# A feed-forward stage in which the rotation of latent keys moves to VectorE in 18 pieces, the norms are spread over three tiles, and the second part of a hidden tile is made in that tile's own turn

## The chip, the cores and the metric

The program runs on one core of a Trainium2 chip. The metric is the device time of one execution in microseconds (us). The engines are TensorE (PE, with its weight loads PEld), VectorE (DVE), ScalarE (ACT), GpSimd (POOL) and the DMA queues of SyncE (SP).

## The reference, cut to what matters

The kernel computes two decoder layers for 16 sequences of 128 tokens with 256 features. Each layer has an attention, a cross attention and a feed-forward part, each followed by an addition and a layer norm:

```python
x = _layernorm(x + _L0_attn_ref(x, ...))
x = _layernorm(x + _L0_xattn_ref(x, ctx_512, ctx_512))
x = _layernorm(x + _L0_ffn_ref(x, w_gate, w_up, w_down, s_gate, s_up, s_down))
x = _layernorm(x + _L1_attn_ref(x, ...))
x = _layernorm(x + _L1_xattn_ref(x, ctx_512, ...))
x = _layernorm(x + _L1_ffn_ref(x, ...))
```

The change is in the third line, the feed-forward of layer 0, whose weights are int8 with a scale for each output column:

```python
gate = silu(x @ w_gate * s_gate)      # 256 -> 1024
up   = x @ w_up * s_up
y    = (gate * up) @ w_down * s_down  # 1024 -> 256
```

While this stage runs, the kernel also prepares an input of a stage far behind it, the fifth line. There the latent context is rotated before it serves as keys and as values:

```python
kv_rope = kv_c * cos[None] + _rotate_half(kv_c) * sin[None]   # 16 x 128 x 64
```

It is made twice, once with the features on the partitions (`mla_keys`, 128 x 2048) and once with the tokens there (`mla_values`, 128 x 1024).

## The kernel before

**Tiles.** `gated_ffn_int8` works in 32 tiles (`TILES`). The sequences form 4 groups of 4 (512 token columns), and the 1024 hidden features form 8 tiles (`FT`) for each group. Tile n has these steps:
- `up(n)` on TensorE (L768): 16 matmuls, 8 for the gate and 8 for up. The input is held as two parts whose sum is x (`x_parts`), so each product is made of two.
- `silu(n)` on ScalarE (L690).
- `fuse(n)` on VectorE (L726): up, scaled, times gate, into one of two buffers `fused`. It reads one operand from PSUM and one from SBUF.
- `hidden_first(n)` on ScalarE (L695): the hidden tile rounded to the matmul's type, the first part of `h_parts`.
- `hidden_second(n)` on VectorE (L731): what the rounding left over, the second part. It reads two operands from SBUF.

**Order of the engines.** Each engine runs its own loop over n, up to `END` = 42, in the order in which it is written, and waits on semaphores. TensorE writes the gate and up products to two PSUM buffers each, so `up(n)` waits for `silu(n - 2)` and `fuse(n - 2)`. ScalarE does `silu(n)`, then `hidden_first(n)`, which waits for `fuse(n)`, and only then `silu(n + 1)`. VectorE does `fuse(n)` and then `hidden_second(n - 1)`, the second part of the tile before.

**Sequences.** When a group's 8 tiles are done, the down product (L780, 16 matmuls of 256 columns) of each of its sequences b is made, one in every second tile: `begins(b)` is 9, 11, 13, ... 39. In VectorE's turn `begins(b) + 1`, an even one, `scale_and_add` scales it (L619), adds the residual (L167), takes the statistics (L171, L172, L173) and forms variance plus epsilon (L174). GpSimd raises that to the power -1/2 (L188), VectorE waits for it and normalises (L181), all in the same turn. GpSimd then adds a bias into `x_tok` (L194), TensorE transposes the normalised rows (L200) and ScalarE copies them to `xT` (L205), these two in their turn `begins(b) + 3`. The last sequence, 15, is finished in the next stage.

**Splits.** For groups 1 to 3 the input's parts are made in tiles 3, 11 and 19 by ScalarE (`split_first`, L685) and at the end of VectorE's turns 4, 12 and 20 (`split_second`, L720).

**What is left of the stage ahead.** In tiles 0 to 4 the last two sequences of the cross attention are finished. In turn 2 VectorE divides and forms the statistics of the last one, in turn 3 it normalises it.

**Rotation.** GpSimd does it after its share of the norms of sequences 0, 1, 2, 4, 6 and 8, in six instructions (L978, L980, L982, L984, L986, L988): `rotate_after(b)`, ahead of which it waits for its own `kept`. The inputs come by DMA into buffers that the cross attention has left.

## Time and profile before

| what | us |
|---|---|
| median of 3 runs | 1135.53 |
| lowest and highest of the 3 | 1128.24, 1140.06 |
| the profiled execution, its own time | 1127.11 |
| its span in the profile | 1125.0 |
| PE busy in the span | 1009.5 |
| DVE busy | 788.7 |
| ACT busy | 556.8 |
| POOL busy | 264.8 |

The profiled execution is a single run, a little under the lowest of the three. A row of the timeline gives the start of an instruction in us from the span's start, its duration, engine, line, operation, output and inputs, and in brackets how long the engine had been idle and what ended that. Durations in neighbouring rows overlap by some hundredths, since an instruction can begin while the one ahead drains. The distance from one start to the next is what an instruction takes from the queue. In the rows `rows` is the home of y, the total and the normalised rows, and `gqa_expT` is the home of gate and fused (and, in its other half, of the rotated copy of the keys).

### The profile page before, as it was taken

The page shows a single profiled execution, that of the slowest core. Times are in us where ns is not written, and L with a number is a line of the kernel's source. Part 1 is how long each engine was busy: PE and PEld are TensorE (multiplying, and loading weights), DVE is VectorE, ACT ScalarE, POOL GpSimd, SP SyncE. Part 2 cuts the span into 40 slices and gives each one's busy share as a digit, 9 for nine tenths or more (in the row PEclk, how much of TensorE's full clock was granted, in tenths as well). Part 3 has the DMA queues.
Part 4 walks back from the last instruction along what each step waited for, and adds up shares of the span by engine and source line. Part 5 has one row for each costly group of instructions (what it writes and reads, how often), then busy time and mean ns, then how long its engine had stood idle before and what let it go on. Part 6 is the DMA issues. An engine that isn't in the chain of part 4 may idle for free. (4 is left out here: it accounts for less than half of the span.)

```text
span 1125.0 us, 23649 instructions
## 1 busy us (share of the span) xinstructions
PE 1009.5 (90%) x8691; PEld 649.9 (58%) x8691; DVE 788.7 (70%) x1959; ACT 556.8 (49%) x1538; POOL 264.8 (24%) x331
## 2 busy tenths in 40 slices
PE   9799989999799999887979788899999998989975
PEld 5466666666333333576755476677777774444432
DVE  2689987898778777577757986744587877723326
ACT  2355436555366667533414264677777774322213
POOL 5301000221111112144331202300000001277843
PEclk9899999999899999999979989999999999999978
DMA  6923433000222221700000006910000002778567
GB/s 191 151 74 104 127 82 114 3 2 3 75 86 91 78 73 57 162 3 1 2 0 2 1 14 226 284 39 17 13 21 20 25 20 76 215 192 228 87 147 264
DMA packets 79197, 94.78 MB, mean 84 GB/s; under 512 B 17504, under 2 KB 61478, under 8 KB 78822
## 3 DMA queue, kind: packets, MB, share of 16 engines
q1 hardware_dynamic: 69356, 78.67, 24.0%
q0 software_dynamic: 6496, 9.57, 4.6%
q10 hardware_dynamic: 3232, 5.03, 1.3%
q8 instruction: 71, 1.16, 0.4%
q14 instruction: 42, 0.34, 0.1%
HBM read 68.65 MB, written 21.97 MB: 81 GB/s over the span
## 5 line engine op out<-in xcount | busy, mean ns | idle before, releaser
L540 DVE TENSOR_REDUCE gqa_x_slots<-banks 128x8 f32<-128x1024 f32 x64 | 78.3, 1225 | 29.5 <-PE banks L434 19.5
L500 ACT ACTIVATE gqa_expT<-banks 128x1024 f32<-128x1024 f32 x64 | 65.5, 1023 | 51.2 <-PE banks L455 51.2
L1735 ACT ACTIVATE mla_probs<-mla_scores,mla_neg_max 128x128 f32<-128x128 f32 x256 | 90.3, 384 | 0.1
L455 PE MATMUL banks<-gqa_x_slotsT,gqa_keys 32*128 32x512 f32 x256 | 73.4, 644 | 13.0 <-issue 4.0
L1808 DVE TENSOR_REDUCE mla_neg_max<-mla_scores 128x8 f32<-128x1024 f32 x32 | 39.2, 1224 | 64.7 <-PE mla_scores L1633 38.4
L434 PE MATMUL banks<-gqa_keys_bd,xT 32*128 32x512 f32 x256 | 72.3, 650 | 1.7 <-PEq L2739 1.4
L768 PE MATMUL banks<-ff_x_parts,ff_w_gate_up 128*128 128x512 f32 x256 | 66.6, 407 | 1.0 <-PEq L358 1.0
L1623 PE MATMUL mla_q_ps<-xT,mla_merged_home 128*128 128x128 f32 x512 | 62.4, 275 | 0.0
L1660 PE MATMUL mla_out_ps<-mla_merged_home,mla_attT 128*128 128x256 f32 x256 | 60.7, 380 | 0.7 <-ACT mla_attT L1749 0.7
L1623 PEld LDWEIGHTS mla_q_ps<-xT,mla_merged_home 128*128 128x128 f32 x512 | 59.7, 192 | 0.0
L1735 ACT ACTIVATION_READ_ACCUMULATOR mla_probs<-mla_scores,mla_neg_max 128x1 f32 x256 | 57.3, 224 | 0.0
L768 PEld LDWEIGHTS banks<-ff_x_parts,ff_w_gate_up 128*128 128x128 f32 x256 | 47.4, 194 | 11.4 <-issue 2.2
L188 POOL TENSOR_TENSOR mla_n_rstd<-mla_n_var_eps,neg_half 128x1 f32<-128x1 f32 x16 | 8.8, 548 | 190.7 <-DVE mla_n_var_eps L174 190.7
L2169 DVE COPY moe_y<-moe_y_ps 112x256 f32<-112x256 f32 x32 | 13.6, 424 | 57.1 <-PE moe_y_ps L2096 38.3
L2924 DVE SCALAR_TENSOR_TENSOR ttt_masked<-banks,ttt_mask 128x512 f32<-128x512 f32 x64 | 43.5, 684 | 12.6 <-PE banks L2845 12.5
L2055 POOL DMA_INDIRECT moe_sums<-moe_y,moe_rows_out x32 | 47.3, 1479 | 17.3 <-issue 8.2
L695 ACT CAST ff_h_parts<-gqa_expT 128x512 fp32r<-128x512 f32 x32 | 19.9, 621 | 62.1 <-DVE gqa_expT L726 62.1
L1660 PEld LDWEIGHTS mla_out_ps<-mla_merged_home,mla_attT 128*128 128x128 f32 x256 | 46.1, 190 | 6.5 <-ACT mla_attT L1749 1.6
L1270 DVE TENSOR_TENSOR bat_prod<-bat_k,ba_attended 128x128 f32<-128x128 f32 (+15 forms) x32 | 40.3, 1318 | 11.6 <-ACT bat_k L1181 7.5
L455 PEld LDWEIGHTS banks<-gqa_x_slotsT,gqa_keys 32*128 32x128 f32 x256 | 21.1, 187 | 46.7 <-issue 46.7
L1640 PEld LDWEIGHTS mla_turned<-ident,mla_probs 128*128 128x128 f32 x256 | 28.4, 141 | 28.1 <-issue 28.1
L2880 PEld LDWEIGHTS banks<-ttt_g_pairs,ttt_masked 128*64 128x64 f32 x1024 | 35.8, 137 | 11.4 <-issue 8.2
(460 smaller groups left out, 2543.8 us busy)
## 6 DMA issues: line engine op xcount, KB each, us to landing
gqa_keys_bd<-in_gqa_keys_bd SPq DMA_DIRECT2D x16, 512.0 KB, 3.2
moe_w_gu<-in_moe_w_gu SPq DMA_DIRECT2D x14, 384.0 KB
moe_w_dn<-in_moe_w_down SPq DMA_DIRECT2D x24, 192.0 KB
moe_sums<-moe_zeros SPq DMA_DIRECT2D x2, 2176.0 KB, 10.3
ba_attended<-in_moe_w_gu SPq DMA_DIRECT2D x10, 384.0 KB
x_tok<-in_mla_kv_wo SPq DMA_DIRECT2D x8, 320.0 KB, 3.7
ttt_by_token<-ttt_g_pairs SPq DMA_DIRECT2D x4, 576.0 KB, 5.1
ttt_lanes<-ttt_by_token SPq DMA_DIRECT2D x16, 144.0 KB
```

The lines of the kernel that those rows point to most:

```text
L434: ins = nc.tensor.matmul(scores[:, j, :], keep["xT"][group, c, b * T:(b + 1) * T], keys_bd[b % NBUF][group, c], start=True, stop=True)
L455: ins = nc.tensor.matmul(scoresT[:, j % 2, :], keys[b % NBUF][group, c, :], x_slotsT[group, k % 2, :], start=True, stop=True)
L500: nc.scalar.activation(expT[:, k % 2, 2 * u:2 * u + 2, :], scoresT, ACT.Exp, scale=HD ** -0.5).then_inc(exp_ready, 1)
L540: nc.vector.tensor_reduce(x_slots[:, b % 2, :, c * NJ + 2 * half:c * NJ + 2 * half + 2, HD].rearrange("p g j -> p j g"), scores[:, of].rea ...
L768: ins = nc.tensor.matmul(tile[:, n % 2], w_up[:, c, k, f * P:(f + 1) * P], x_parts[:, g % 2, part, c, :], start=(c == 0 and part == 0), st ...
L1270: tt(prod[:, u % PB, 0:l + 1, :], k[:, c, 0:l + 1, :], q[:, c, l, :].unsqueeze(1).to_broadcast([P, l + 1, T]), ALU.mult).then_inc(prod_rea ...
L1623: ins = nc.tensor.matmul(q_ps[:, i, :], to_keys[:, c, 2 * pair:2 * pair + 2, :], keep["xT"][:, c, b * T:(b + 1) * T], start=(c == 0), stop ...
L1660: ins = nc.tensor.matmul(out_ps, attT[:, k % 2, i, :], to_out[:, r * QP + i, :], start=(r == 0 and i == 0), stop=(r == UNITS - 1 and i == ...
L1735: ins = nc.scalar.activation(probs[:, k % NB, e, i, :], scores[:, k % 2, e, i, :], ACT.Exp, bias=neg_max[:, k % 2, e, i:i + 1], accum_out= ...
L1808: nc.vector.tensor_reduce(neg_max[:, k % 2], scores[:, k % 2], AX_X, ALU.max, negate=True).then_inc(max_kept, 1)
L2055: nc.gpsimd.indirect_dma_start(sums, bass.IndirectOffsetOnAxis(ap=rows_out[0:USED, s:s + 1], axis=0), y2[0:USED, s % 4, :], None, compute_ ...
L2924: stt(masked[:, u % NB].rearrange("p n j i -> p (n j) i"), scores[:, u % NB].rearrange("p n j i -> p (n j) i"), 1.0, mask[:].unsqueeze(1). ...
```

## The change

Four things are different, all in `gated_ffn_int8` and `LatentWeights`:
- GpSimd no longer rotates, and no longer waits for `kept` behind each norm. `LatentWeights.rotate` does it on VectorE in 18 pieces of 128 x 512 elements, one in each of the turns 11 to 28: twelve for the keys (cosine product, sine product, sum, for four sequences each) and six for the values.
- For sequences 0 to 11 (`LATE` = 12) the norm is spread over three turns of VectorE. Turn `begins + 1`: scale and add. Turn `begins + 2`: statistics, and the variance at its end. Turn `begins + 3`: normalise. The piece of the rotation and the second part stand between steps that depend on each other. Sequences 12 to 14 keep the whole norm in one turn.
- `hidden_second(n)` is in turn n, behind `fuse(n)`, and not in turn n + 1.
- The transposition on TensorE and the copy on ScalarE of sequences 0 to 11 come one turn later, in `begins + 4`, behind the down product of a later sequence. TensorE's row of transposition then stands between a down product and two tiles of `up`.

```diff
         def _(pool):
-            rotate_after = latent.gpsimd(pool)
...
                 norm.gpsimd(pool, b)
-                pool.wait_ge(norm.kept, b + 1)
-                rotate_after(b)
...
+        LATE = B - 4
+        turned_at = lambda n: next((b for b in range(B - 1) if begins(b) + (4 if b < LATE else 3) == n), None)
...
-                if sequence_at(n - 3) is not None:
-                    norm.scalar(act, sequence_at(n - 3))
+                if turned_at(n) is not None:
+                    norm.scalar(act, turned_at(n))
...
+            ROTATE_AT = FT + 3
+
+            def normalise(b):
+                need(dve, norm.rstd_ready, b + 1)
+                need(dve, norm.kept, b)
+                need(dve, norm.turn_ready, b)
+                nc.vector.tensor_scalar(norm.normed, norm.total, norm.mean_var[:, 0:1], norm.rstd[:], ALU.subtract, ALU.mult).then_inc(norm.norm_ready, 1)
...
-                b = sequence_at(n - 1)
+                b, was, before = (None if sequence_at(n - k) == B - 1 else sequence_at(n - k) for k in (1, 2, 3))
...
-                if 1 <= n <= TILES:
-                    hidden_second(n - 1)
...
-                    last.scale_and_add(dve, order, b, down[b % 2])
+                if before is not None and before < LATE:
+                    normalise(before)
+                if b is not None:
+                    dve.wait_ge(down_ready, b + 1)
+                    if b:
+                        order.after(added)
+                    nc.vector.tensor_tensor(last.y, down[b % 2], last.s_down[:], ALU.mult).then_inc(y_ready, 1)
+                if was is not None and was < LATE:
+                    order.after(added)
+                    summed = order.mark(nc.vector.bn_stats(norm.stats[:], norm.total))
+                if n == ROTATE_AT:
+                    dve.wait_ge(fetched, LOADS)
+                if ROTATE_AT <= n < ROTATE_AT + latent.PIECES:
+                    latent.rotate(dve, n - ROTATE_AT)
+                if was is not None and was < LATE:
+                    order.after(summed)
+                    nc.vector.memset(norm.spare[:], 0.0)
+                    spread = order.mark(nc.vector.bn_aggr(norm.mean_var[:], norm.stats[:]))
+                if b is not None:
...
+                    added = order.mark(norm.added(b, last.y))
+                if n < TILES:
+                    hidden_second(n)
+                if was is not None and was < LATE:
+                    order.after(spread)
+                    nc.vector.tensor_scalar(norm.var_eps[:], norm.mean_var[:, 1:2], LN_EPS, None, ALU.add).then_inc(norm.var_ready, 1)
+                if b is not None and b >= LATE:
+                    order.after(added)
+                    norm.vector_stats(order)
+                    normalise(b)
...
-                if b is not None and b < B - 1:
-                    norm.vector_end(dve, b)
+            dve.wait_ge(latent.roped, latent.PIECES)
...
-                if sequence_at(n - 3) is not None:
-                    norm.tensor(pe, sequence_at(n - 3))
+                if turned_at(n) is not None:
+                    norm.tensor(pe, turned_at(n))
...
+    PIECES = 18
+
+    def rotate(self, eng, k):
...
+        if k < 12:
+            some, whole, turned = slice(k // 3 * 4, k // 3 * 4 + 4), kvT[:], rolledT
...
+        if k % 3 == 0:
+            tt(whole[:, some], whole[:, some], cos, ALU.mult).then_inc(self.roped, 1)
+        elif k % 3 == 1:
+            tt(turned[:, some], turned[:, some], sin, ALU.mult).then_inc(self.roped, 1)
+        else:
+            eng.wait_ge(self.roped, k)
+            tt(out[:, some], whole[:, some], turned[:, some], ALU.add).then_inc(self.roped, 1)
```

On VectorE, turns 12 and 13 read so before. The rows with `rows`, `ff_n_stats` and `ff_n_mean_var` are the norm of sequence 1, L720 is the split of group 2.

```order
943 L726 SCALAR_TENSOR_TENSOR gqa_expT<-banks,ff_s_in,gqa_expT 128x512
944 L731 TENSOR_TENSOR ff_h_parts<-gqa_expT,ff_h_parts 128x512
945 L619 TENSOR_TENSOR rows<-banks,ff_s_down 128x256
946 L167 TENSOR_TENSOR rows<-rows,x_tok 128x256
947 L171 BN_STATS ff_n_stats<-rows 128x6
948 L172 MEMSET ff_n_spare 128x1
949 L173 BN_AGGR ff_n_mean_var<-ff_n_stats 128x2
950 L174 TENSOR_SCALAR ff_n_var_eps<-ff_n_mean_var 128x1
951 L720 TENSOR_TENSOR ff_x_parts<-xT,ff_x_parts 128x1024
952 L181 TENSOR_SCALAR rows<-rows,ff_n_mean_var,ff_n_rstd 128x256
953 L726 SCALAR_TENSOR_TENSOR gqa_expT<-banks,ff_s_in,gqa_expT 128x512
954 L731 TENSOR_TENSOR ff_h_parts<-gqa_expT,ff_h_parts 128x512
```

The same two turns with the change. L739 normalises sequence 0, L755 scales sequence 1, L758 to L777 are its statistics, L1018 and L1021 are pieces of the rotation.

```order
945 L725 SCALAR_TENSOR_TENSOR gqa_expT<-banks,ff_s_in,gqa_expT 128x512
946 L739 TENSOR_SCALAR rows<-rows,ff_n_mean_var,ff_n_rstd 128x256
947 L755 TENSOR_TENSOR rows<-banks,ff_s_down 128x256
948 L1018 TENSOR_TENSOR gqa_expT<-gqa_expT,mla_sinT 128x512
949 L167 TENSOR_TENSOR rows<-rows,x_tok 128x256
950 L730 TENSOR_TENSOR ff_h_parts<-gqa_expT,ff_h_parts 128x512
951 L719 TENSOR_TENSOR ff_x_parts<-xT,ff_x_parts 128x1024
952 L725 SCALAR_TENSOR_TENSOR gqa_expT<-banks,ff_s_in,gqa_expT 128x512
953 L758 BN_STATS ff_n_stats<-rows 128x6
954 L1021 TENSOR_TENSOR mla_keys<-mla_keys,gqa_expT 128x512
955 L765 MEMSET ff_n_spare 128x1
956 L766 BN_AGGR ff_n_mean_var<-ff_n_stats 128x2
```

Five steps that depend on each other (L619 to L181) stood in one turn; now they are in three, and each has a foreign instruction between itself and the one that it needs.

In turns 2 to 4 on VectorE, where the cross attention's last norm (`gqa_n`) is made, the rows before were:

```order
907 L726 SCALAR_TENSOR_TENSOR gqa_expT<-banks,ff_s_in,gqa_expT 128x512
908 L731 TENSOR_TENSOR ff_h_parts<-gqa_expT,ff_h_parts 128x512
909 L341 RECIPROCAL gqa_rsum<-banks 128x16
910 L344 TENSOR_TENSOR gqa_attended<-banks,gqa_rsum 128x32 x4
911 L167 TENSOR_TENSOR gqa_n_total<-gqa_attended,x_tok 128x256
```

With the change they are:

```order
909 L725 SCALAR_TENSOR_TENSOR gqa_expT<-banks,ff_s_in,gqa_expT 128x512
910 L730 TENSOR_TENSOR ff_h_parts<-gqa_expT,ff_h_parts 128x512
911 L341 RECIPROCAL gqa_rsum<-banks 128x16
912 L344 TENSOR_TENSOR gqa_attended<-banks,gqa_rsum 128x32 x4
913 L167 TENSOR_TENSOR gqa_n_total<-gqa_attended,x_tok 128x256
```

The rows read alike, but L731 there was the second part of tile 1, and L730 here is that of tile 2, whose first part ScalarE has still to make.

## Rows read from the trace of the kernel before

**Rows 1.** Windows: span, busy time (instructions) of each engine, granted clock, DMA.

```profile
456.00:582.00 126.00, 103.99 (x562) 85.88 (x562) 88.71 (x189) 48.61 (x86) 45.95 (x40) 0.95 0.18 37
567.00:571.00 4.00, 3.86 (x18) 3.86 (x19) 2.01 (x8) 0.00 (x0) 1.29 (x2) 0.50 0.00 0
```

**Rows 2.** Groups by line in 456 to 582 us: busy, mean ns, idle before.

```profile
L731 DVE TENSOR_TENSOR ff_h_parts<-gqa_expT,ff_h_parts 128x512 fp32r<-128x512 f32 x32 | 31.2, 976 | 0.1
...
L205 ACT COPY xT<-banks 128x256 f32<-128x256 f32 x17 | 6.3, 368 | 12.9 <-PE banks L200 12.9
...
L720 DVE TENSOR_TENSOR ff_x_parts<-xT,ff_x_parts 128x1024 fp32r<-128x1024 f32 x3 | 3.6, 1216 | 0.0
L685 ACT CAST ff_x_parts<-xT 128x1024 fp32r<-128x1024 f32 x3 | 3.1, 1043 | 0.0
```

**Rows 3.** Timeline of tile 6 and the start of tile 7.

```profile
475.27 0.75 DVE L726 SCALAR_TENSOR_TENSOR gqa_expT<-banks,ff_s_in,gqa_expT 128x512 f32<-128x512 f32 x1 [0.68 <-ACT gqa_expT L690]
...
476.06 0.62 ACT L695 CAST ff_h_parts<-gqa_expT 128x512 fp32r<-128x512 f32 x1 [0.82 <-DVE gqa_expT L726]
476.58 0.69 ACT L690 ACTIVATE gqa_expT<-banks,ff_s_in 128x512 f32<-128x512 f32 x1
477.30 0.75 DVE L726 SCALAR_TENSOR_TENSOR gqa_expT<-banks,ff_s_in,gqa_expT 128x512 f32<-128x512 f32 x1 [0.68 <-ACT gqa_expT L690]
```

**Rows 4.** Timeline, DVE and POOL, from turn 10 into turn 12.

```profile
484.79 0.75 DVE L726 SCALAR_TENSOR_TENSOR gqa_expT<-banks,ff_s_in,gqa_expT 128x512 f32<-128x512 f32 x1 [2.08 <-PE banks L768]
...
485.45 0.68 DVE L731 TENSOR_TENSOR ff_h_parts<-gqa_expT,ff_h_parts 128x512 fp32r<-128x512 f32 x1
...
486.05 0.42 DVE L619 TENSOR_TENSOR rows<-banks,ff_s_down 128x256 f32<-128x256 f32 x1
...
486.50 0.42 DVE L167 TENSOR_TENSOR rows<-rows,x_tok 128x256 f32<-128x256 f32 x1
486.96 0.43 DVE L171 BATCH_NORM_STATS2 ff_n_stats<-rows 128x6 f32<-128x256 f32 x1
487.43 0.18 DVE L173 BATCH_NORM_AGGREGATE ff_n_mean_var<-ff_n_stats 128x2 f32<-128x6 f32 x1
...
487.64 0.15 DVE L174 TENSOR_SCALAR ff_n_var_eps<-ff_n_mean_var 128x1 f32<-128x1 f32 x1
...
488.53 0.41 DVE L181 TENSOR_SCALAR rows<-rows,ff_n_mean_var,ff_n_rstd 128x256 f32<-128x256 f32 x1 [0.73 <-POOL ff_n_rstd L188]
488.98 0.75 DVE L726 SCALAR_TENSOR_TENSOR gqa_expT<-banks,ff_s_in,gqa_expT 128x512 f32<-128x512 f32 x1
489.02 0.75 POOL L194 TENSOR_TENSOR x_tok<-rows,bat_b_out 128x256 f32<-128x256 f32 x1 [0.53 <-DVE rows L181]
...
489.85 4.97 POOL L978 TENSOR_TENSOR mla_keys<-mla_keys,mla_cosT 128x2048 f32<-128x2048 f32 x1
...
492.62 2.74 DVE L731 TENSOR_TENSOR ff_h_parts<-gqa_expT,ff_h_parts 128x512 fp32r<-128x512 f32 x1
```

**Rows 5.** Timeline in turn 36, late in the stage.

```profile
574.00 0.74 POOL L194 TENSOR_TENSOR x_tok<-rows,bat_b_out 128x256 f32<-128x256 f32 x1 [0.53 <-DVE rows L181]
...
574.42 0.61 DVE L167 TENSOR_TENSOR rows<-rows,x_tok 128x256 f32<-128x256 f32 x1
```

**Rows 6.** Timeline of PE: the down products of sequences 0, 5, 6 and 12.

```profile
480.73 2.14 PE L780 MATMUL banks<-ff_w_down,ff_h_parts 128*128 128x256 f32 x16 [1.30 <-DVE ff_h_parts L731]
...
519.88 2.02 PE L780 MATMUL banks<-ff_w_down,ff_h_parts 128*128 128x256 f32 x16
...
525.66 2.02 PE L780 MATMUL banks<-ff_w_down,ff_h_parts 128*128 128x256 f32 x16
...
567.14 3.79 PE L780 MATMUL banks<-ff_w_down,ff_h_parts 128*128 128x256 f32 x16 [1.47 <-DVE ff_h_parts L731]
```

**Rows 7.** Timeline of DVE: `fuse(29)`, and products of another stage.

```profile
558.74 0.75 DVE L726 SCALAR_TENSOR_TENSOR gqa_expT<-banks,ff_s_in,gqa_expT 128x512 f32<-128x512 f32 x1
...
606.55 4.68 DVE L1270 TENSOR_TENSOR bat_prod<-bat_k,ba_attended 128x896 f32<-128x896 f32 x4
```

More of the change, by code:

```diff
@@ L740, in _ @@
                     fuse(n)
[L741 to L746 removed]
+                if before is not None and before < LATE:
[17 more added lines that the diff above has]
+                if b is not None:
+                    if b == 0:
+                        dve.wait_ge(cross.norm.kept, B)
+                    dve.wait_ge(y_ready, b + 1)
+                    need(dve, norm.norm_ready, b)
+                    added = order.mark(norm.added(b, last.y))
[8 more added lines that the diff above has]
+                    normalise(b)
                 if n == 2:
@@ L753, in _ @@
                     split_second(group_to_split(n - 1))
-                if b is not None and b < B - 1:
-                    norm.vector_end(dve, b)
+            dve.wait_ge(latent.roped, latent.PIECES)
         @block.tensor
@@ L966, in open @@
         return loads
[L968 removed]
+    PIECES = 18
+    def rotate(self, eng, k):
         nc, DC = self.nc, self.DC
         kvT, rolledT, kv, rolled, cosT, sinT, cosines, sines = self.parts
[L971 to L990 removed]
+        tt = nc.vector.tensor_tensor
+        if k < 12:
+            some, whole, turned = slice(k // 3 * 4, k // 3 * 4 + 4), kvT[:], rolledT
+            out, cos, sin = self.keys, cosT[:].unsqueeze(1).to_broadcast([P, 4, T]), sinT[:].unsqueeze(1).to_broadcast([P, 4, T])
+        else:
+            some, whole, turned = slice((k - 12) // 3 * 8, (k - 12) // 3 * 8 + 8), kv, rolled
+            out, cos, sin = self.values, cosines[:].unsqueeze(1).to_broadcast([P, 8, DC]), sines[:].unsqueeze(1).to_broadcast([P, 8, DC])
+        if k % 3 == 0:
+            tt(whole[:, some], whole[:, some], cos, ALU.mult).then_inc(self.roped, 1)
+        elif k % 3 == 1:
+            tt(turned[:, some], turned[:, some], sin, ALU.mult).then_inc(self.roped, 1)
+        else:
+            eng.wait_ge(self.roped, k)
+            tt(out[:, some], whole[:, some], turned[:, some], ALU.add).then_inc(self.roped, 1)
 def batch_axis_attention(nc, keep, io, inputs, latent, ffn, banks, attended):
```

21 lines of the change are left out of this document (1 added, 20 removed).

## Prediction

> **What bounds the kernel now.** I first read the windows over the stage that the change touches, 456 to 582 us. TensorE is busy 104.0 of 126.0 us and VectorE 88.7, so neither is full [rows 1]. What ends the waits has to be read tile by tile. In a plain tile, with no norm in it, the order is `fuse`, 0.79 us later ScalarE's first part, 0.52 later `silu` of the next tile, 0.72 later the next `fuse`: 2.03 us a tile, a loop between ScalarE and VectorE that the change leaves as it is [rows 3]. In the steady part the work comes in pairs of tiles, with one down product in each. TensorE alone needs 5.78 us for a pair: that is the step between two down products where it ran without a gap (519.88 to 525.66) [rows 6]. But from `fuse(11)` at 488.98 [rows 4] to `fuse(29)` at 558.74 [rows 7] nine pairs took 69.76 us, 7.75 each. The bound is VectorE's queue and what it waits for there. Two things stand in it. The whole norm is in one turn, with 0.73 us idle until GpSimd's power is back [rows 4]. And the second part of a tile, 0.68 us when undisturbed, took 2.74 us when it met GpSimd's rotation: that ran from 489.85 to 494.82, and the second part, begun at 492.62, ended 0.54 behind it [rows 4]. Over the stage the mean is 976 ns in place of some 680, so the 32 of them lost 9.5 us [rows 2].
>
> **A pair of turns with the change.** Steps from start to start [rows 4]: fuse 0.67 (from tiles where the second part follows), second part 0.60, scale 0.45, add 0.46, statistics 0.47, aggregate 0.21, normalise 0.45. The variance is a 0.15 us record; with the overlap of 0.08 that the fuse shows (0.75 against 0.67) I take 0.07. A piece has the shape of the second part, two SBUF operands of 512 elements, so 0.60. The nearest row with a broadcast operand is the attention's, 4.68 us for four of 896 elements: 1.17 each, and 512/896 of it 0.67 [rows 7]. So a piece costs 0.60 to 0.67.
> - Even turn: fuse, normalise, scale, piece, add, second part: 0.67 + 0.45 + 0.45 + 0.60 + 0.46 + 0.60 = 3.23.
> - Odd turn: fuse, statistics, piece, aggregate, second part, variance: 0.67 + 0.47 + 0.60 + 0.21 + 0.60 + 0.07 = 2.62. The second part can start 0.79 + 0.62 + 0.03 = 1.44 after the fuse [rows 3] and its place comes at 1.95, so it doesn't wait.
>
> Two waits stay. From the variance's start to the normalisation is 0.89 us [rows 4]; only 0.07 and a fuse of 0.67 lie between, so 0.15 is left of the 0.73. And GpSimd's bias addition ends 1.24 us after the normalisation began (488.53 to 489.77) [rows 4], while the piece begins at 0.90. In turn 36 an addition on VectorE with two SBUF operands, begun 0.42 after such a GpSimd addition, took 0.61 in place of 0.42 and ended 0.29 behind its end [rows 5]. So such an operation needs GpSimd to be done 0.13 after its start, and the piece loses 1.24 - 1.03 = 0.21. Pair: 3.23 + 2.62 + 0.15 + 0.21 = 6.21 us, 0.43 above TensorE's 5.78. Bounds: 5.85 if both waits vanish (then TensorE's 5.78 is close behind), and 6.35 with pieces of 0.67.
>
> The Trainium skill (SBUF — State Buffer, Who interferes with whom) says that a VectorE instruction with two SBUF inputs contends with a GpSimd instruction that reads SBUF, and that whichever issues first has the pair for its whole length. The 2.74 us row agrees. It speaks against this change too: each of the 18 pieces is such an instruction and meets the short additions that stay on GpSimd. By the rule the loss is the 0.21 of the sum where GpSimd is first; where the piece is first, GpSimd's addition waits, and no one needs that soon.
>
> **Moved steps that cost.** The second part in its own turn waits for ScalarE from 0.67 to 1.44 behind the fuse. In a plain tile that is free: 1.44 + 0.60 = 2.04 against the loop's 2.03. Where something follows it, that something is 0.77 later: in turn 2 the cross attention's division and statistics, in front of `fuse(3)`; in turn 4 the split of group 1, in front of `fuse(5)`. So `fuse(5)` and all plain tiles to 9 come 1.54 later. The second part of tile 7, though, no longer stands behind `fuse(8)`: it ends at 477.30 + 1.54 + 0.02 + 1.44 + 0.68 = 480.98, and the first down product starts at 481.03, against 480.73 with its 1.30 us of waiting before [rows 3, 6]. The start of the stage thus loses 0.3 us: `fuse(10)` 484.79 becomes 485.09.
>
> **The sum.** Turn 10 has no normalisation and no piece: 0.67 + 0.45 + 0.46 + 0.60 = 2.18, `fuse(11)` at 487.27. `fuse(12)` follows TensorE: one pair without its transposition (5.78 - 0.2 = 5.5) after `fuse(10)`, 490.6. Turn 12: 3.23 + 0.21 + the split's 1.21 - 0.08 [rows 2] = 4.57, `fuse(13)` at 495.2. From here VectorE is the bound: 8 pairs of 6.21, the second split 1.13, and in turn 19 ScalarE's cast (1.04) and copy (0.37) between first part and `silu` [rows 2]: `fuse(20)` not before 1.31 + 0.95 + 0.27 + 0.72 = 3.25 in place of 2.62 + 0.15, 0.48 more. 49.7 + 1.1 + 0.5 = 51.3: `fuse(29)` at 546.5, before 558.74. Turns 29 and 30 have no piece: 2.11 and 2.99 with the two waits, `fuse(31)` at 551.6; its second part ends 2.12 later, and the down product of sequence 12 starts at 553.75 against 567.14 [rows 6]: 13.4 us earlier. Behind it the order is nearly that of before, one norm in a turn, and I leave the tail as it is. TensorE has 3 to 4 us with nothing to do ahead of that product, as it had before (the product then took 3.79 us at a granted clock of 0.50, the 1.2 GHz level, against 2.02 at the full 2.4 GHz [rows 1, 6]), so I count on no gain of clock. At full clock it would be 1.8 more.
>
> GpSimd loses about 23 us of work, worth nothing beyond the stalls counted. The rotation's results are first read more than 100 us later. Profiled execution: 1127.1 - 13.4 = 1113.7. That execution was 8.4 us under the median of the three runs. On the median the same difference gives 1135.5 - 13.4 = **1122.1 us**, 1.2% less. A measurement of this kernel tells about 1% (11.4 us) from no change.
>
> **Rivals.**
> - *TensorE becomes the bound* (0.17). The two waits of a pair vanish, since GpSimd's addition and the pieces meet less than I think, and the tail runs at full clock: 8.5 x 0.36 + 1.8 = 4.9 more, 1117. For it: TensorE's gaps in the middle almost close, so its clock stays up. Against: both waits are worked out from rows.
> - *Smaller gain, VectorE fuller than counted* (0.19). A piece that loses GpSimd's whole addition (0.74 in place of 0.21) makes a pair 6.74, nine pairs 4.8 us; and in turn 4 TensorE waits about 3.1 us, 1.54 more than before, for the cross attention's last norm, which may drop its clock for a tile or two, 1 to 2 us. 13.4 - 6.4 = 7: 1128.5. For it: the count leaves no slack in nine pairs. Against: the addition of turn 36 lost only the overlap.
> - *Slower: TensorE's clock falls* (0.04). With VectorE as the bound TensorE has a gap of 0.43 us in each pair. If the clock fell to the lower level in the middle part, a pair would take 5.78 x 3.79 / 2.02 = 10.8 us, 4.6 more than 6.21; three such pairs use up the gain, and eight make it 1159. Against: TensorE was idle 17% of the stage before, at a mean granted clock of 0.95 [rows 1]; now it is idle less.
> - *The change doesn't reach the end* (0.04). The next stage would have to begin on something other than the last transposition, a transfer say; 1135. The stage moved 37 GB/s on the mean, with a DMA share of 0.18 [rows 1], and nothing of it lies near its end.
>
> The Trainium skill (TensorE: Matmul & The Clock Gate, HAM oscillation) warns that frequent small gaps between groups of matmuls can make the clock swing between its levels. That is the mechanism of the slower rival, put beside it here; the one row that shows the lower level follows gaps of microseconds, not of 0.4.
>
> **Numbers.** Forecast case 0.56, rivals 0.17, 0.19, 0.04, 0.04. The forecast's own spread is 1117 to 1127: pieces at 0.67 cost 1.2, waits gone give 3, and the median of a few runs moves by some us (1128 to 1140 before). Four fifths of it and all of the first rival are beyond 1%: faster 0.63. The small gain and the case that doesn't reach the end are mostly within 1%: same 0.31. Slower by over 1%: 0.06. The range takes in the first two rivals with the runs' spread: 1112 to 1131.
>
> **What would show it.** Second parts all near 0.68 us, none at 2 or 3. The idle time ahead of the normalisation near 0.15 in the spread turns and 0.73 in the last three. `fuse` to `fuse` over two tiles near 6.2 us in turns 13 to 29, with VectorE's idle time nearly gone and TensorE waiting for `fuse`. `fuse(5)` some 1.5 us later than before. Pieces of 0.68 us, every second one about 0.9. The down product of sequence 12 starts near 553.7. The prediction is wrong if pieces take over 1 us, if ScalarE (waiting for a transposition that now comes later) holds back `silu`, or if the granted clock in 490 to 550 is below 0.9.

## The result, and the profile after

| what | before | after |
|---|---|---|
| median, us | 1132.22 (4 runs, 1128.24 to 1140.06) | 1112.83 (4 runs, 1112.50 to 1113.81) |
| profiled execution, own time | 1127.11 | 1112.94 |
| its span | 1125.0 | 1111.1 |
| ratio | | 0.9864, 95% interval 0.9831 to 0.9896 |

The change makes the kernel faster, by 1.0 to 1.7%. The ratio compares undisturbed runs, which are the lower ones of before; the medians alone would give 0.983.

The page of the kernel after, engines and their share of the span:

```profile
span 1111.1 us, 23660 instructions
...
PE 1000.8 (90%) x8691; PEld 646.1 (58%) x8691; DVE 790.2 (71%) x1977; ACT 557.4 (50%) x1538; POOL 240.1 (22%) x325
```

VectorE's busy time is nearly what it was (788.7), though the rotation came to it: the stalls left as the pieces came.

To compare stages I take the stage from its first gate product to the first product of the next stage. It was 455.99 to 582.93 = 126.9 us and is 458.76 to 568.83 = 110.1: **16.9 us shorter**. The span fell by only 13.9, mainly since the stage began 2.8 us later. The code ahead of the stage is the same in both kernels; what is known of the later start stands under `b_again` below. From here on times are compared within the stage. Windows of the kernel after: the whole stage, and a part of its steady middle (columns as in [rows 1]).

```profile
458.76:568.83 110.07, 98.74 (x562) 83.60 (x563) 89.94 (x207) 48.66 (x87) 21.23 (x34) 0.98 0.21 43
499.00:515.00 16.00, 16.00 (x98) 14.23 (x97) 15.99 (x37) 7.78 (x15) 3.88 (x6) 1.00 0.00 1
```

In the middle both TensorE (16.00 of 16) and VectorE (15.99) are full. The groups by line, against those of [rows 2]:

```profile
L730 DVE TENSOR_TENSOR ff_h_parts<-gqa_expT,ff_h_parts 128x512 fp32r<-128x512 f32 x32 | 21.6, 676 | 7.1 <-ACT ff_h_parts L694 6.9
...
L739 DVE TENSOR_SCALAR rows<-rows,ff_n_mean_var,ff_n_rstd 128x256 f32<-128x256 f32 x15 | 6.2, 411 | 3.4 <-POOL ff_n_rstd L188 3.3
```

The second parts are at 676 ns (976 before). The idle time ahead of the normalisation is 3.4 us for 15 of them, not 0.73 each. Nearly all of it stands ahead of the last five, sequences 10 to 14, with 0.66 or 0.67 each. Sequences 10 and 11 are spread too, but in turns 32 and 34 no tile is left whose `fuse` could fill the wait.

One pair of turns, the timeline of the kernel after, VectorE with GpSimd's two rows. It answers to [rows 4].

```profile
500.25 0.73 DVE L725 SCALAR_TENSOR_TENSOR gqa_expT<-banks,ff_s_in,gqa_expT 128x512 f32<-128x512 f32 x1
500.40 0.55 POOL L188 TENSOR_TENSOR ff_n_rstd<-ff_n_var_eps,neg_half 128x1 f32<-128x1 f32 x1 [5.03 <-DVE ff_n_var_eps L777]
...
500.99 0.41 DVE L739 TENSOR_SCALAR rows<-rows,ff_n_mean_var,ff_n_rstd 128x256 f32<-128x256 f32 x1
...
501.31 0.42 DVE L755 TENSOR_TENSOR rows<-banks,ff_s_down 128x256 f32<-128x256 f32 x1
501.48 0.75 POOL L194 TENSOR_TENSOR x_tok<-rows,bat_b_out 128x256 f32<-128x256 f32 x1 [0.53 <-DVE rows L739]
...
501.65 1.13 DVE L1016 TENSOR_TENSOR mla_keys<-mla_keys,mla_cosT 128x512 f32<-128x512 f32 x1
...
502.70 0.41 DVE L167 TENSOR_TENSOR rows<-rows,x_tok 128x256 f32<-128x256 f32 x1
...
503.03 0.68 DVE L730 TENSOR_TENSOR ff_h_parts<-gqa_expT,ff_h_parts 128x512 fp32r<-128x512 f32 x1
503.64 0.74 DVE L725 SCALAR_TENSOR_TENSOR gqa_expT<-banks,ff_s_in,gqa_expT 128x512 f32<-128x512 f32 x1
504.30 0.41 DVE L758 BATCH_NORM_STATS2 ff_n_stats<-rows 128x6 f32<-128x256 f32 x1
...
504.63 0.67 DVE L1018 TENSOR_TENSOR gqa_expT<-gqa_expT,mla_sinT 128x512 f32<-128x512 f32 x1
...
505.23 0.17 DVE L766 BATCH_NORM_AGGREGATE ff_n_mean_var<-ff_n_stats 128x2 f32<-128x6 f32 x1
505.25 0.06 DVE L765 MEMSET ff_n_spare<- 128x1 f32 x1
505.32 0.65 DVE L730 TENSOR_TENSOR ff_h_parts<-gqa_expT,ff_h_parts 128x512 fp32r<-128x512 f32 x1
505.90 0.14 DVE L777 TENSOR_SCALAR ff_n_var_eps<-ff_n_mean_var 128x1 f32<-128x1 f32 x1
505.97 0.73 DVE L725 SCALAR_TENSOR_TENSOR gqa_expT<-banks,ff_s_in,gqa_expT 128x512 f32<-128x512 f32 x1
```

Read from start to start (for the statistics to the piece behind them, for the aggregation to the second part behind it): normalise 0.32, scale 0.34, add 0.33, statistics 0.33, where the prediction had 0.45 to 0.47 for each; the aggregation 0.09, not 0.21. The piece that meets GpSimd's addition takes 1.05 (0.81 predicted): it could start after 0.66 us and not 0.90 behind the normalisation, so it waited longer for an addition that ended when predicted (1.24 behind it). Like the second part of before, it ended 0.55 us behind GpSimd (502.78 against 502.23). The pair is 5.72 us, not 6.21.

TensorE over the same time, where the down product comes in every second tile (against [rows 6]):

```profile
500.79 2.03 PE L814 MATMUL banks<-ff_w_down,ff_h_parts 128*128 128x256 f32 x16
502.66 0.38 PE L200 MATMUL banks<-ident,rows 128*128 128x128 f32 x2
502.79 3.93 PE L802 MATMUL banks<-ff_x_parts,ff_w_gate_up 128*128 128x512 f32 x16
506.56 2.03 PE L814 MATMUL banks<-ff_w_down,ff_h_parts 128*128 128x256 f32 x16
```

5.77 us for a pair: the engines need the same time, and TensorE has no gap. The 16 matmuls of L802 are those of two tiles, 8 for each (4 for the gate, 4 for up); the 16 per tile in the description of the kernel before are wrong, there too it is 8 (256 in the stage). No sum of the prediction uses that count.

### The profile page after: what moved, and what is told of

Its sections match the earlier page's. It is cut to its first block and busy times, and to the rows that moved or that the text cites. A ratio compares the mean times of both kernels' runs of the same rounds, so it can differ in the third digit from the quotient of the medians.

```text
span 1111.1 us, 23660 instructions
## 1 busy us (share of the span) xinstructions
PE 1000.8 (90%) x8691; PEld 646.1 (58%) x8691; DVE 790.2 (71%) x1977; ACT 557.4 (50%) x1538; POOL 240.1 (22%) x325
## 3 DMA queue, kind: packets, MB, share of 16 engines
q1 hardware_dynamic: 69356, 78.67, 24.7%
## 5 line engine op out<-in xcount | busy, mean ns | idle before, releaser
L1839 DVE TENSOR_REDUCE mla_neg_max<-mla_scores 128x8 f32<-128x1024 f32 x32 | 39.2, 1224 | 64.7 <-PE mla_scores L1664 38.4
L802 PE MATMUL banks<-ff_x_parts,ff_w_gate_up 128*128 128x512 f32 x256 | 63.1, 397 | 1.4 <-PEq L358 1.0
L802 PEld LDWEIGHTS banks<-ff_x_parts,ff_w_gate_up 128*128 128x128 f32 x256 | 46.6, 188 | 12.4 <-issue 2.2
```

What stands on the lines that cost most here:

```text
L802: ins = nc.tensor.matmul(tile[:, n % 2], w_up[:, c, k, f * P:(f + 1) * P], x_parts[:, g % 2, part, c, :], start=(c == 0 and part == 0), st ...
L1839: nc.vector.tensor_reduce(neg_max[:, k % 2], scores[:, k % 2], AX_X, ALU.max, negate=True).then_inc(max_kept, 1)
```

## The experiments

"Stage" is the length defined above, from one profiled execution. R stands for the rotation moved to VectorE, S for the spread norms, O for the second part in its own turn.

| kernel | R S O | stage, us | own time, us |
|---|---|---|---|
| before | - - - | 126.9 | 1127.1 |
| `b_again` | - - - | 127.0 | 1126.6 |
| `b_pieces` | R - - | 121.5 | 1123.1 |
| `b_spread` | - S - | 123.6 | 1131.1 |
| `b_own_turn` | - - O | 130.1 | 1131.5 |
| `a_next_turn` | R S - | 111.1 | 1108.1 |
| `a_unspread` | R - O | 118.5 | 1116.8 |
| `a_pool` | - S O | 125.0 | 1129.0 |
| after | R S O | 110.1 | 1112.9 |
| `b_no_rotation` | no rotation, - - | 116.8 | 1119.1 |
| `a_no_rotation` | no rotation, S O | 108.1 | 1109.6 |
| `a_waits` | R S O, waits added | 118.8 | 1116.7 |
| `a_head` | R S, O from tile 5 | 108.5 | 1106.0 |
| `a_all` | `a_head` and three more | 107.8 | 1107.6 (median of 6) |

**The kernel before once more (`b_again`).** No edit.

> The kernel before, unchanged, profiled a second time. The length of the feed-forward stage (from the first gate matmul to the first matmul of the next stage) was 126.9 us before and 110.1 with the change, yet the span fell by 13.9 only, since the stage began 2.8 us later. If that later start is not the change's, this run shows a stage of 126.9 us within 0.5 and a start anywhere between 455 and 460 us. If the change itself moved the start, this run begins at 456.0 again.

The stage was 127.0, so a single profile gives its length well. It began at 456.2 again, while in the kernel after it began at 458.8. By the expectation's own sign that would put the later start down to the change. But `a_head`, which has nearly the whole change, starts at 455.7. Over all kernels the start lies between 455.7 and 460.5 and goes with TensorE's mean granted clock up to there, in code that is the same in all: by the clock records of the traces it is 0.981 in the five that start at 455.7 to 456.3, 0.974 to 0.978 in the six at 457.7 to 458.8, and 0.966 to 0.970 in the three from 459.8 on. Much of the difference lies in the cross attention. Before, after and `a_all` in 300 to 350 us:

```profile
300.00:350.00 50.00, 45.20 (x321) 17.70 (x320) 37.38 (x89) 31.66 (x43) 5.60 (x13) 0.95 0.22 72
```
```profile
300.00:350.00 50.00, 43.04 (x292) 16.65 (x292) 33.51 (x79) 28.48 (x39) 5.60 (x13) 0.92 0.19 55
```
```profile
300.00:350.00 50.00, 44.26 (x281) 16.57 (x279) 32.77 (x77) 27.73 (x37) 4.86 (x11) 0.85 0.17 53
```

The clock is the third number from the end: 0.95, 0.92, 0.85, with fewer matmuls done in the same 50 us, and the stage starts at 456.0, 458.8 and 460.2. What sets the clock off there wasn't settled, nor whether it goes with the kernel or with the single execution: `a_unspread` and `a_head` start like before, `a_waits` like after. Behind the stage the code is the same again, and took between 536.4 us (`a_next_turn`) and 545.3 (`b_spread`). All that lies outside the stage adds up to 995 to 1006 us, 998 before and 1001 after. So own times of single runs differ by up to 10 us that can't be put down to an edit, and I judge the edits by the stage.

**No rotation at all, before (`b_no_rotation`).** A GpSimd fill of the values stands in the rotation's place; nothing is rotated.

```diff
+            nc.gpsimd.memset(latent.values[:], 0.0).then_inc(latent.roped, 1)
...
-                rotate_after(b)
```

> The kernel before with the rotation of the latent keys and values left out (the values are only cleared). Theory: the rotation on GpSimd costs VectorE's second parts 9.5 us of stalls and delays GpSimd's power once or twice, so the stage takes 116 to 118 us in place of 126.9. Rival, GpSimd's relief explains the whole gain: 112 us or less.

116.8: the rotation on GpSimd, which nobody waits for in this stage, cost the stage 10.1 us. The second parts are at 682 ns there.

The 10.1 us can hold more than VectorE's stalls. In the kernel before TensorE's clock fell behind waits that follow from them. Timeline of PE, and a window:

```profile
499.08 0.44 PE L200 MATMUL banks<-ident,rows 128*128 128x128 f32 x2 [3.08 <-DVE rows L181]
499.27 3.16 PE L768 MATMUL banks<-ff_x_parts,ff_w_gate_up 128*128 128x512 f32 x8
```
```profile
500.00:503.40 3.40, 3.40 (x12) 2.85 (x12) 2.72 (x3) 2.53 (x5) 3.40 (x1) 0.50 0.00 0
```

TensorE was idle for 3.08 us, and soon after it worked at a granted clock of 0.50, the 1.2 GHz level: a tile took 3.16 us, where it takes 2.0 at full clock. A second such stretch is at 513.6 to 517.1. In its first 95 us the stage of the kernel without the rotation has none, and that after the change none either. An estimate from the two stretches, 6.9 us at half speed, is that up to 3.4 of the 10.1 us are the clock's; the runs don't separate the two parts.

**The rotation's move alone (`b_pieces`).** `latent.rotate` in VectorE's turns 11 to 28, norms and second parts as before.

```diff
-                rotate_after(b)
...
+                if FT + 3 <= n < FT + 3 + latent.PIECES:
+                    latent.rotate(dve, n - FT - 3)
```

> The kernel before with only the rotation moved: 18 pieces on VectorE in turns 11 to 28, behind the second part of the tile before; norms in one turn and second parts as before. Theory: the 9.5 us of stalls go, 18 x 0.60 = 10.8 us of work come onto the engine that sets the pace, so the stage stays at 125 to 128 us: moving the rotation gains nothing alone. Rival, the move itself is the gain: 112 to 117 us.

121.5: a gain of 5.4 us, more than my theory's. The 18 pieces cost 4.7 over no rotation, though they hold VectorE for 18 times 0.60 = 10.8. The rest went into time in which VectorE had waited: ahead of `fuse` it waits 9.5 us for ScalarE in the stage, and 15.5 without the rotation.

**The own turn alone (`b_own_turn`).**

```diff
-                if 1 <= n <= TILES:
-                    hidden_second(n - 1)
...
                     last.scale_and_add(dve, order, b, down[b % 2])
+                if n < TILES:
+                    hidden_second(n)
```

> The kernel before with only the second part of a tile made in its own turn, between the variance and the normalisation. Theory: it fills 0.6 of the 0.73 us that VectorE waits for GpSimd's power, 0.4 to 0.6 us in each of 11 pairs, less 0.4 at the start of the stage: 121 to 124 us, with the second parts that meet the rotation still at 2 to 4 us. Rival, only the spread norms help: 126 to 127.5 us.

130.1: wrong by its sign. Timeline of VectorE and GpSimd in turn 11:

```profile
495.25 0.75 DVE L726 SCALAR_TENSOR_TENSOR gqa_expT<-banks,ff_s_in,gqa_expT 128x512 f32<-128x512 f32 x1
...
496.11 4.61 POOL L978 TENSOR_TENSOR mla_keys<-mla_keys,mla_cosT 128x2048 f32<-128x2048 f32 x1
496.69 4.59 DVE L731 TENSOR_TENSOR ff_h_parts<-gqa_expT,ff_h_parts 128x512 fp32r<-128x512 f32 x1 [0.69 <-ACT ff_h_parts L695]
```

In the order of before, tile 10's second part had begun just ahead of GpSimd's instruction, and tile 11's stood behind `fuse(12)`, which had to wait itself: 2.8 of GpSimd's 4.97 us had gone by when it began [rows 4]. In its own turn tile 11's second part starts 0.58 us after GpSimd and stands for nearly the whole length. The mean of the 32 is 1211 ns.

The 130.1 is too high for the edit, though. The granted clock was 0.51 in the first 3.3 us of the stage and 0.50 from 476.7 to 480.1. `fuse(10)` stands at 31.6 us in the stage; in the kernel after, with the same order of the engines up to there, it stands at 29.2. So some 127.8 would be fair: a loss of 0.8 us, where my theory had a gain of 3 to 6.

**All but the move (`a_pool`).** The kernel after with the rotation on GpSimd.

```diff
-                    latent.rotate(dve, n - ROTATE_AT)
...
+                rotate_after(b)
```

> The changed kernel with the rotation back on GpSimd in its six long instructions; norms spread, second parts in their own turn. Theory: VectorE loses 18 pieces but its operations with two SBUF operands meet the long instructions again, some 9 us of stalls in one piece each, of which the slack between the engines hides part: the stage takes 111 to 117 us against 110.1. Rival, the move of the rotation carries most of the gain: over 120 us.

125.0, the rival's. Timeline in turn 12:

```profile
494.37 4.66 POOL L1010 TENSOR_TENSOR mla_keys<-mla_keys,mla_cosT 128x2048 f32<-128x2048 f32 x1
494.49 5.08 DVE L733 TENSOR_TENSOR ff_h_parts<-gqa_expT,ff_h_parts 128x512 fp32r<-128x512 f32 x1
```

GpSimd's long instruction starts 1.3 us behind the normalisation. It does so in the kernel before too (488.53 to 489.85) [rows 4]; what differs is which step of VectorE comes next. With the normalisation first in its turn, two-operand steps are next, and lose all of it. The second part ended 0.54 us behind GpSimd (499.57 against 499.03), as in [rows 4].

**The spreading alone (`b_spread`).** `a_pool` with the second part in the next turn.

> The kernel before with the norms of sequences 0 to 11 spread over three turns and nothing else: the rotation is on GpSimd, the second part of a tile is in the next turn. It is the one combination of the three edits that is missing. Stage lengths so far: before 126.9, rotation moved 121.5, own turn 130.1, moved and spread 111.1, spread and own turn 125.0, all three 110.1. My theory is that a second part in the next turn falls behind fuse, where GpSimd's long instruction, begun behind the norm's power, is already well on its way, as in the kernel before, so that the losses stay about 9 us, and that the spreading still gives its 8 on the waits for the power and on dependent steps: 117 to 121. The rival (GpSimd's instruction and the second part then start together, as with all but the move, 5 us each) gives 123 to 127.

123.6, in the rival's range. The start was disturbed here by 1.3 us (its first down product came 26.1 us into the stage, before it was 24.7), so 122.2 would be fair, which lies between my theory and the rival; either way it is more than I expected. Timeline in turn 12:

```profile
498.73 4.65 POOL L1010 TENSOR_TENSOR mla_keys<-mla_keys,mla_cosT 128x2048 f32<-128x2048 f32 x1
```
```profile
498.86 5.61 DVE L722 TENSOR_TENSOR ff_x_parts<-xT,ff_x_parts 128x1024 fp32r<-128x1024 f32 x1
```

My theory looked at second parts only (mean 941 ns). The split of the input is such an instruction too, and lost 4.4 us each, twice.

**The norms unspread (`a_unspread`).**

```diff
-        LATE = B - 4
+        LATE = 0
```

> The changed kernel with LATE = 0: every norm in one turn, transpositions in the turn of before; pieces on VectorE and second parts in their own turn stay. Theory: each pair pays the 0.66 to 0.73 us wait for GpSimd's power and about 0.12 us for each step that waits for the one in front of it, so a pair takes 6.7 to 7.0 us in place of 5.7 and the stage 119 to 123 us. Rival, the order of the norm's steps is worth little: 110 to 113 us.

118.5, just under the range: spreading is worth 8.4 us here, and 10.5 between `b_pieces` and `a_next_turn`. The start was disturbed here too: at a granted clock of 0.50 from 472.3 to 475.6 the first down product came at 26.1 us in the stage (25.1 in the kernel after), so 117.5 and a worth of 7.5 would be fair.

**The second part in the next turn (`a_next_turn`).**

```diff
+                if 1 <= n <= TILES:
+                    hidden_second(n - 1)
...
-                if n < TILES:
-                    hidden_second(n)
```

> The changed kernel with the second part of a tile again in the next turn, behind that turn's fuse. Theory: pairs stay near 5.8 us, since VectorE's work is the same; the start of the stage is 1.5 us quicker to fuse(5), but the down products wait again for the second part of a group's last tile (1.3 us for the first one), so 109 to 111.5 us. Rival, the own turn is part of the gain: over 113 us.

111.1: the own turn is worth 1.0 us. Its pair is 5.81 us.

**No rotation, after (`a_no_rotation`).** No piece on VectorE, the same GpSimd fill; nothing is rotated.

> The changed kernel with the rotation left out (the values are only cleared). If VectorE still sets the pace, the stage falls by several us, to 104 to 107. If TensorE has become the bound in the middle part, as its 16.0 us busy of 16 from 499 to 515 us suggest, it falls by less than 2.5 us (107.5 to 109.5), and that from turns 12, 20 to 24 and the end alone.

108.1. Windows:

```profile
499.00:515.00 16.00, 16.00 (x98) 14.21 (x97) 13.74 (x33) 8.45 (x15) 3.72 (x7) 1.00 0.00 1
```

VectorE fell from 15.99 to 13.74, TensorE stayed full, and the stage gained only 2.0: in the middle TensorE is a bound of its own (from one down product to the next it takes 5.77 us here as well), and the pieces are nearly free.

**Waits for the neighbour (`a_waits`).** The same instructions in the same order, with a wait for the step directly ahead before most steps of a spread turn.

```diff
+                    need(dve, norm.norm_ready, b)
                     nc.vector.tensor_tensor(last.y, down[b % 2], last.s_down[:], ALU.mult).then_inc(y_ready, 1)
...
+                    if b is not None:
+                        dve.wait_ge(y_ready, b + 1)
+                    if was is not None and was < LATE:
+                        order.after(summed)
                     latent.rotate(dve, n - ROTATE_AT)
+                    dve.wait_ge(latent.roped, n - ROTATE_AT + 1)
```

> The change, with waits added on VectorE's own semaphores so that each step of a spread turn waits for the end of the step directly ahead of it. The work and the order are the same. The theory on the mis-sized term is that a step takes 0.33 us from the queue where it doesn't wait for its neighbour and 0.45 where it does (scale, add, normalise, statistics), and that this is why a pair of turns took 5.7 and not 6.2 us. It expects a pair of 6.1 to 6.4, TensorE waiting again, and a stage of 113 to 116 (the prediction's sum gives 113.5). The rival (the steps are short for another reason, such as the tile they read being idle, or TensorE sets the pair at 5.78 anyway) gives a stage of 110 to 111.

The theory's side, and beyond its range: a pair of 6.76 us and a stage of 118.8. I had counted the waits at the four steps of the norm, but the kernel has them at ten. Timeline:

```profile
501.24 0.75 DVE L725 SCALAR_TENSOR_TENSOR gqa_expT<-banks,ff_s_in,gqa_expT 128x512 f32<-128x512 f32 x1
502.02 0.41 DVE L739 TENSOR_SCALAR rows<-rows,ff_n_mean_var,ff_n_rstd 128x256 f32<-128x256 f32 x1
502.57 0.42 DVE L757 TENSOR_TENSOR rows<-banks,ff_s_down 128x256 f32<-128x256 f32 x1
503.03 0.77 DVE L1030 TENSOR_TENSOR mla_keys<-mla_keys,mla_cosT 128x512 f32<-128x512 f32 x1
503.83 0.43 DVE L167 TENSOR_TENSOR rows<-rows,x_tok 128x256 f32<-128x256 f32 x1
504.30 0.69 DVE L730 TENSOR_TENSOR ff_h_parts<-gqa_expT,ff_h_parts 128x512 fp32r<-128x512 f32 x1
504.90 0.75 DVE L725 SCALAR_TENSOR_TENSOR gqa_expT<-banks,ff_s_in,gqa_expT 128x512 f32<-128x512 f32 x1
505.75 0.43 DVE L761 BATCH_NORM_STATS2 ff_n_stats<-rows 128x6 f32<-128x256 f32 x1
506.22 0.69 DVE L1032 TENSOR_TENSOR gqa_expT<-gqa_expT,mla_sinT 128x512 f32<-128x512 f32 x1
```

From start to start: scale 0.46, add 0.47, statistics 0.47 (0.34, 0.33 and 0.33 in the kernel after), piece 0.73 (0.60, to the aggregation at 506.95). The durations are within 0.02. Where the next step has no new wait, from the second part to `fuse`, it is 0.60 in both. And the piece that meets GpSimd's addition starts 1.01 us behind the normalisation and takes 0.80, not 1.05: of what the quicker steps win in the kernel after, 0.25 us is lost again at this piece. TensorE waits again (14.96 of 16 us in the window shown of the others).

**The start (`a_head`).**

```diff
+            OWN = 5
...
+                if 1 <= n < OWN:
+                    hidden_second(n - 1)
...
-                if n < TILES:
+                if n == OWN:
+                    hidden_second(n - 1)
+                if OWN <= n < TILES:
                     hidden_second(n)
```

> The change, with the second part of a tile in the next turn for tiles 0 to 4 and in its own turn from tile 5 on. The prediction put the loss of the own turn at 1.54 us at fuse(5) and only 0.3 at the first down product. The theory expects fuse(5) 1.5 us earlier in the stage (17.3 in place of 18.8), the first down product and fuse(10) 1.2 to 1.6 earlier, and a stage of 108.5 to 109.5. The rival (the start is given back before the pairs, since fuse(12) waits for something else) gives 109.8 to 110.3.

As the theory has it: `fuse(5)` at 17.2 us in the stage (18.8), the first down product at 23.5 (25.1), the stage 108.5.

**Put together (`a_all`).** `a_head`, and: ScalarE's split ahead of the first part in tiles 11 and 19; the scale of the next sequence between variance and normalisation in the last turns; all transpositions in `begins + 4`.

```diff
+                if n > SPLIT_AT and group_to_split(n):
+                    split_first(group_to_split(n))
                 if n < TILES:
                     hidden_first(n)
...
                     norm.vector_stats(order)
+                    if b + 1 < B - 1:
+                        scale(b + 1)
                     normalise(b)
```

> What the runs point to, put together: the change with the second parts of tiles 0 to 4 in the next turn, ScalarE's split of the input ahead of the first part in tiles 11 and 19 (where fuse waited 1.00 and 0.83 us for ScalarE behind it), the scale of the next sequence hoisted into the wait for the power in the last turns, and all transpositions in begins + 4. The theory expects 1.0 to 1.5 us from the start, 0.5 to 1.8 from the split and 0.5 to 1.0 from the tail: a stage of 106 to 108, against 110.1, and a time of 1107 to 1111, 1.7 to 2.3 per cent under the kernel before. The rival (TensorE bounds the pairs, so only the start and the tail count, and the later start of some kernels takes it back) gives a stage of 108.5 to 110 and no measurable difference from the change.

Stage 107.8. Against the kernel before, in one series: median 1107.58 us (6 runs, 1102.54 to 1110.08) to 1126.02 (11 runs, 1120.64 to 1133.42), ratio 0.9825, interval 0.9785 to 0.9864. It has the shortest stage of the study, but its interval meets that of the change (0.9831 to 0.9896), and the two weren't timed in one series, so no lead of it over the change is shown in device time. In the stage it is 2.3 us shorter. Where the parts went: the start gave 1.6. The split gave 0.9 in turn 19 and nothing in turn 11: `fuse(12)` stood at 33.1 us in the stage with it and without it, since `silu` then waited for TensorE. The tail gave nothing: from the down product of sequence 12 to the next stage it took 16.3 us, and 16.1 in `a_head`. Timeline of its tail and, below, of the tail after the change:

```profile
554.68 0.43 DVE L749 TENSOR_TENSOR rows<-banks,ff_s_down 128x256 f32<-128x256 f32 x1
555.42 0.41 DVE L741 TENSOR_SCALAR rows<-rows,ff_n_mean_var,ff_n_rstd 128x256 f32<-128x256 f32 x1 [0.31 <-POOL ff_n_rstd L188]
555.93 0.99 DVE L167 TENSOR_TENSOR rows<-rows,x_tok 128x256 f32<-128x256 f32 x1
```
```profile
556.49 0.41 DVE L739 TENSOR_SCALAR rows<-rows,ff_n_mean_var,ff_n_rstd 128x256 f32<-128x256 f32 x1 [0.67 <-POOL ff_n_rstd L188]
556.81 0.41 DVE L755 TENSOR_TENSOR rows<-banks,ff_s_down 128x256 f32<-128x256 f32 x1
557.26 0.73 DVE L167 TENSOR_TENSOR rows<-rows,x_tok 128x256 f32<-128x256 f32 x1
```

The hoisted scale fills the wait for the power (0.31 idle in place of 0.67), the addition then starts 0.51 us behind the normalisation in place of 0.77, and takes 0.99 in place of 0.73: it ends 1.50 behind the normalisation in both. It reads two SBUF operands and waits for GpSimd's bias addition, which hangs on that same normalisation. A turn of the tail is 3.05 us in both.

## Why the prediction was right, and where it was off

The direction, the place and the mechanism hold, but the pair of turns was counted too long. The median of 1112.83 lies in the range near its lower end, 9 us under the forecast of 1122.

- **What bounds the kernel.** Right. The second parts lost 9.5 us to GpSimd by the rows, and leaving the rotation out gave back 10.1. That the two are so near may be in part luck, since the 10.1 can hold a loss of clock as well (`b_no_rotation`). What the prediction didn't see is that this price hangs on the order around it: without the move, the other two edits together gained 1.9 us, since the steps behind the normalisation then ran into GpSimd's instruction from its start.
- **The start.** Right within a tenth: `fuse(5)` 1.55 us later in the stage (1.54), the first down product 0.33 (0.3), `fuse(10)` 0.39 (0.3). `a_head` shows by its gain that it is the own turn's price.
- **Turns 10 to 13.** Right: `fuse(13)` 39.2 us into the stage, both predicted and measured. The row for `fuse(12)` names ScalarE, with its split ahead of `silu`, but `a_all` took the split away from there and `fuse(12)` didn't move: it is TensorE, as predicted.
- **The pair of turns.** This is the term that was mis-sized, 6.21 us against 5.72. I took the steps' lengths from a turn in which each waits for the one directly ahead (0.45 to 0.47), for turns in which none does, where they are 0.33. Four steps and the aggregation are 0.63 less, the piece that meets GpSimd's addition 0.24 more, the wait for the power 0.07 and not 0.15. From `fuse(13)` to `fuse(29)` it took 47.7 us, where the prediction had 51.3: 3.6 less, and with it the 3.5 us by which the stage beat the forecast of 13.4. `a_waits` shows the cause: with waits at ten steps the pair is 6.76. With the shorter pair VectorE isn't the only bound of the middle, as the prediction had it: TensorE is full there too.
- **Turn 19.** `fuse(20)` waited 0.83 us for ScalarE, where 0.48 over the usual 0.15 was predicted; `a_all` gives 0.9 for taking it away.
- **From there to the end.** From `fuse(29)` to the down product of sequence 12 it took 7.16 us (7.25 by the prediction), and from there to the next stage 16.07, where before it was 15.79.
- **TensorE's clock.** No fall, so the slower rival didn't come: the stage's mean rose from 0.94 to 0.98, with 1.00 in 490 to 550 us. The gap of 0.43 us in each pair, from which that rival argued, wasn't there either. In `a_waits`, where TensorE has gaps again (14.96 of 16 us), the clock in the window shown is 1.00 as well. The prediction counted on no gain of clock, and overlooked the stretches at 0.50 in the middle of the stage before, which are gone; what part of the 16.9 us is theirs isn't separated. It put the full clock in the tail at 1.8 us: no run shows that. In `a_head` the granted clock from the down product of sequence 12 to the next stage is 1.00, after the change 0.86, and both take 16.07 us.
- **The rival of TensorE as the bound** had the outcome nearly right (1117) and the reason wrong. The wait for GpSimd's addition didn't vanish but doubled, from the 0.21 of the prediction to 0.45; the pair fell to TensorE's 5.77 because of the shorter steps.
- **What would show it.** The second parts (676 ns), the small idle time ahead of the spread normalisations (0.07 us a pair; 0.66 in the tail, ahead of five and not three), pieces of 0.67 with every second one longer: seen, the longer one 1.13 and not 0.9. "Pieces over 1 us" was one of the signs of being wrong, and every second piece has it. It was that same wait that was counted too small there, while the steps around it took less than counted. The down product of sequence 12 was forecast 13.4 us earlier, and came 17.15 us earlier within the stage. TensorE waiting for `fuse` in every pair: not seen.

Against the span the sum looks better than it was: 13.9 us measured for 13.4 predicted, of which the stage made 16.9 and its late start took 2.8. That the forecast of 1113.7 for the profiled execution came so near to its 1112.94 is luck: a pair that was counted too long and a start that nobody foresaw cancel out. On the medians the fall is 19.4. The forecast on that basis started from a median of three runs, 1135.5, that lay 12 us apart; a fourth run brought it to 1132.2.

The edits are far from additive: alone they give 5.4 (R), 3.4 (S) and -3.2 us (O), 5.6 in sum (9.3 if the two disturbed starts are taken off); together 16.9. The move and the spreading carry it (15.9 together without O). Each removes what would eat the other's gain: the spread steps run into GpSimd's long instruction unless it is gone, and the pieces add to a full turn unless the norm's waits are out of it.

## What to carry to other kernels

When the length of a step is taken from a trace, look whether it waited for its neighbour on its own engine: a short instruction behind an independent one takes less from the queue, and spreading dependent steps gains that beside the waits that one sees. When two edits work on the same engine, price the second in the order that the first leaves: what the long GpSimd instructions cost here hung on which two-operand VectorE instruction came right behind their start. When an engine waits long, look at its clock behind the wait: in the kernel before a wait of 3.08 us was followed by TensorE's work at half clock. And before an instruction is hoisted into a wait, see what the step behind the wait meets: in the tail here it met GpSimd's own addition, and the gain was nil.

## What the runs showed of the hardware

**A wait on the neighbour costs about 0.12 us of VectorE's queue.** Instructions of 128 x 256 with the same duration (0.41 to 0.43) take 0.33 us from start to start where the next instruction doesn't depend on them, and 0.45 to 0.47 where the next one waits for them; those of 128 x 512 take 0.60 and 0.73. Two of the steps in `a_waits` lost 0.2 (statistics behind `fuse`, 0.66 to 0.85; scale behind normalise, 0.32 to 0.55); why these lost more is open. The Trainium skill (VectorE: DVE Perf Modes, The DRAIN you can't avoid) says that a semaphore after each of eight copies added nothing and that the flush comes anyway. The rows here don't agree for these instructions: the same work with the waits took 6.76 us a pair and without them 5.72. The same section adds that a next instruction which isn't held starts earlier, and with that the 0.33 us agree, for instructions recorded at 0.41. The page's copies weren't run here.

**VectorE and GpSimd hold each other up for whole instructions.** VectorE instructions with two SBUF operands of 512 elements ended a fixed time behind GpSimd's, however long they had stood: 0.54 us for the second part behind 4.66, 0.55 for a piece behind 0.75. It works the other way too: GpSimd's 2048 elements took 4.61 to 4.66 us where VectorE came second, and 4.97 in [rows 4], where a second part that VectorE had begun at 489.65 was still running:

```profile
489.65 0.68 DVE L731 TENSOR_TENSOR ff_h_parts<-gqa_expT,ff_h_parts 128x512 fp32r<-128x512 f32 x1
```

The Trainium skill (SBUF — State Buffer, Who interferes with whom) names it a lock that the first comer holds, on the ports to SBUF that the two share; the rows agree, and `b_spread` adds that the split of the input is hit as well (5.61 us in place of 1.2).
